# A macaron block on one core: the longest attention row turned by 32x32 squares and DMA instead of on TensorE

## The reference, cut to what matters

```python
x = x + 0.5 * ffn(layernorm(x))
x = x + attn(layernorm(x))
x = x + 0.5 * ffn(layernorm(x))

def attn(h):                       # h: 8 x 512 x 512
    q = h @ w_q.T                  # 16 heads of 32
    k, v = split(h @ w_kv.T)       # one key and one value head of 32 for all
    q, k = rotate(q / sqrt(32)), rotate(k / sqrt(32))
    p = softmax(where(causal, -inf, q @ k.T))
    return (p @ v) @ w_proj.T + b_proj
```

## Time and profile before

| what | value |
|---|---|
| median of three runs | 2725.27 us |
| profiled execution, time | 2725.83 us |
| profiled execution, span | 2724.0 us |
| granted TensorE clock, mean | 0.999 |
| TensorE busy | 2686.4 us, 99% |
| VectorE busy | 1877.6 us, 69% |
| ScalarE busy | 1117.9 us, 41% |
| GpSimd busy | 305.9 us, 11% |
| attention, first to last step | 1089.8 to 1660.0 us |

### The profile page before, as it was taken

The page is one execution under the profiler, slowest core; times in us unless marked ns, Lnnn a source line. Parts: engine busy times, 40 slices in busy tenths (PEclk is TensorE's granted clock), DMA queues, the critical chain, the costliest instruction groups (busy, mean ns, idle before and its releaser), DMA issues.

```text
span 2724.0 us, 41269 instructions
## 1 busy us (share of the span) xinstructions
PE 2686.4 (99%) x15328; PEld 2170.4 (80%) x15328; DVE 1877.6 (69%) x3538; ACT 1117.9 (41%) x2376; POOL 305.9 (11%) x318
## 2 busy tenths in 40 slices
PE   8999999999999999999999999999999999999999
PEld 6888888888888887677777767888888888888887
DVE  6667766766686667777777775667766776677655
ACT  4333333333333333877777774333333333333332
POOL 0000000000000004544444420000000000000000
PEclk9999999999999999999999999999999999999999
DMA  4211411331132111000000012212321242123100
GB/s 141 88 49 56 162 47 46 95 123 47 46 124 93 47 46 59 20 17 27 30 32 29 29 56 86 81 50 78 112 78 58 70 135 82 46 60 126 47 16 31
DMA packets 96747, 181.63 MB, mean 67 GB/s; under 512 B 7744, under 2 KB 32576, under 8 KB 96320
## 3 DMA queue, kind: packets, MB, share of 16 engines
q1 hardware_dynamic: 96576, 179.34, 19.6%
HBM read 141.56 MB, written 37.75 MB: 66 GB/s over the span
## 4 chain that ended last, share of the span: by engine, by line
PE 94%; DVE 4%; ACT 1%; POOL 1%; issue 1%; DMA 0%; SPq 0%; DVEq 0%; ACTq 0%; POOLq 0%
PE bank L457 50%; PE bank L478 25%; PE bank L1199 5%; PE bank L1167 3%; PE bank L1190 3%; PE bank L1214 3%; PE bank L1227 3%; DVE probs L1449 1%; PE bank L1142 1%; PE bank L1175 1%; PE bank L335 1%; POOL xnt_l L1072 0%; DVE pt L1455 0%; PE bank L494 0%; DVE att L1468 0%
## 5 line engine op out<-in xcount | busy, mean ns | idle before, releaser
L457 PE MATMUL bank<-xnt_h,wgu_h 128*128 128x512 f32 x2048 | 799.0, 390 | 4.4 <-ACT sg L575 2.8
L457 PE MATMUL bank<-xnt_h,wgu_l 128*128 128x512 f32 x2048 | 797.6, 389 | 1.0 <-issue 1.0
L457 PE MATMUL bank<-xnt_l,wgu_h 128*128 128x512 f32 x2048 | 797.7, 390 | 0.0
L650 DVE TENSOR_TENSOR h<-bank,sg 128x512 f32<-128x512 f32 x256 | 176.7, 690 | 544.1 <-PE bank L457 530.4
L457 PEld LDWEIGHTS bank<-xnt_h,wgu_h 128*128 128x128 f32 x2048 | 385.0, 188 | 87.3 <-ACT sg L575 3.7
L457 PEld LDWEIGHTS bank<-xnt_h,wgu_l 128*128 128x128 f32 x2048 | 385.0, 188 | 80.1
L457 PEld LDWEIGHTS bank<-xnt_l,wgu_h 128*128 128x128 f32 x2048 | 385.1, 188 | 79.6
L579 ACT ACTIVATE mag<-h 128x512 f32<-128x512 f32 x256 | 162.0, 633 | 674.5 <-DVE h L650 674.5
L478 PE MATMUL bank<-wd_h,hs_h 128*128 128x512 f32 x1008 | 392.2, 389 | 0.0
L478 PE MATMUL bank<-wd_h,hs_l 128*128 128x512 f32 x1008 | 392.1, 389 | 0.0
L478 PE MATMUL bank<-wd_l,hs_h 128*128 128x512 f32 x1008 | 392.1, 389 | 0.0
(11 more groups left out here) (137 smaller groups left out, 3196.5 us busy)
## 6 DMA issues: line engine op xcount, KB each, us to landing
raw_gu<-in_w_gu SPq DMA_DIRECT2D x128, 512.0 KB, 4.9
raw_d<-in_w_d SPq DMA_DIRECT2D x128, 256.0 KB, 2.6
x_mid<-x_sb SPq DMA_DIRECT2D x64, 256.0 KB, 2.1
x_squares<-xs SPq DMA_DIRECT2D x48, 256.0 KB, 3.9
xs<-x_squares SPq DMA_DIRECT2D x12, 1024.0 KB, 5.6
x_sb<-x_mid SPq DMA_DIRECT2D x10, 1024.0 KB, 5.5
x_sb<-in_x SPq DMA_DIRECT2D x32, 256.0 KB, 4.2
out<-x_sb SPq DMA_DIRECT2D x32, 256.0 KB, 2.1
```

What stands on the lines that cost most here:

```text
L457: last = pe.matmul(ps, w[:, r, kind, k], xs[:, b, k], start=(i == 0), stop=(i == 3 * KD - 1))
L650: v.tensor_tensor(h[:, r], bank[UP + r % 2][:, :], sg[:, r % 2], ALU.mult).then_inc(h_done, 1)
```

## The change

Row 3, the longest, becomes the first of each group (`ORDER` is 3, 0, 1, 2, and the unit of row 3 is at steps 0, 4, 8 and 12). Its blocks are no longer turned on TensorE and copied. VectorE writes its masked scores to `probs3` in pieces of 32 columns, turns the 32x32 squares of two heads at a time in place (`turn_squares`), and the tile goes to DRAM (`squares`) in four transfers of 256 KB and comes back in one of 1 MB as `pt3`. Two of the four are issued by SyncE and two by ScalarE. ScalarE waits for both turns and, from the second group on, for the previous read back before it issues. SyncE issues the read after all four have landed and after the previous group's weighing.

The other three rows get a buffer each. VectorE does all four masks first in a step, and copies one block a group instead of four; ScalarE copies five instead of six. TensorE weighs once a group, in the step of the next long row. Some projections, statistics and the turn of the keys stand in other steps. GpSimd splits x tiles earlier in a step. SyncE's stores and loads of x are woven between the groups. In the second phase `inside` is called after the first gate and after the first up bank, with the last weighing at the first and the last output projections at the second.

```diff
+    squares = nc.dram_tensor("squares", [S // 32, 32, TT, HG * 32], F32, kind="Internal").ap()
...
-    pt = place("pt", [P, 2 * TT, HG, P], F32)
+    pt = place("pt", [P, 6, HG, P], F32)
+    probs1 = place("probs1", [P, HG, 2 * P], F32)
...
-    probs = place("probs", [P, 3, HG, S], F32)
+    probs3 = place("probs3", [P, S // 32, HG, 32], F32)
+    pt3 = place("pt3", [P, TT, TT, HG, 32], F32)
+    probs2 = place("probs2", [P, HG, 3 * P], F32)
+    probs0 = place("probs0", [P, HG, P], F32)
...
-                            if inside and r == kind == 0:
+                            if inside and r == 0:
...
-            ORDER = (0, 1, 2, 3)
-            PLACES = ((7,), (5, 6), (0, 1, 2), (3, 4, 5, 6))
-            ON_VECTOR = ((), (1,), (1,), (1, 3))
-            TURN_X, TURN_KV, TURN_K = {11: 0, 12: 1, 13: 2, 14: 3}, 1, 4
+            ORDER = (3, 0, 1, 2)
+            LONG = 3
+            PLACES = ((0,), (1, 2), (3, 4, 5))
+            ON_VECTOR = ((), (), (1,))
+            probs_of = (probs0, probs1, probs2)
+            TURN_X, TURN_KV, KEYS, TURN_K = {11: 0, 12: 1, 13: 2, 14: 3}, 1, 8, 10
...
-            FIRST_PROJECT = {0: ("kv", 0), 1: ("q", 0), 5: ("q", 1), 9: ("q", 2), 10: ("q", 3)}
-            LAST_PROJECT = {2: ("out", 0), 5: ("out", 1), 9: ("out", 2), 13: ("out", 3)}
-            STATS = {3: 0, 5: 1, 7: 2, 8: 3}
+            FIRST_PROJECT = {0: ("kv", 0), 2: ("q", 0), 5: ("q", 1), 6: ("q", 2), 10: ("q", 3)}
+            LAST_PROJECT = {2: ("out", 0), 6: ("out", 1), 10: ("out", 2), 14: ("out", 3)}
+            STATS = {3: 0, 4: 1, 5: 2, 7: 3}
...
+            def store_squares(engine, a):
+                engine.dma_start(squares[:, :, a].rearrange("c i x -> i c x"),
+                                 probs3[a * 32:(a + 1) * 32, :, :, :].rearrange("p c s n -> p c (s n)")).then_inc(squares_stored, 16)
...
+                def turn_long(G):
+
+                    if G > 0:
+                        sp.wait_ge(pt3_loaded, G * 16)
+                    sp.wait_ge(squared, (G + 1) * 2)
+                    for a in range(TT // 2):
+                        store_squares(sp, a)
+                    sp.wait_ge(squares_stored, (G + 1) * TT * 16)
+                    if G > 0:
+                        sp.wait_ge(pv_done, G)
+                    sp.dma_start(pt3[:, :, :, :, :].rearrange("p j a s n -> p j (a s n)"),
+                                 squares.rearrange("(j q) i a x -> (q i) j (a x)", q=TT)).then_inc(pt3_loaded, 16)
...
+                for B in range(BATCHES):
+                    for hg in range(NHG):
+                        turn_long(B * NHG + hg)
...
+                    if B > 0:
+                        store(B - 1)
+                    if 0 < B < BATCHES - 1:
+                        sp.wait_ge(ax_stored, B * TT * 16)
+                        load(B + SLOTS - 1)
...
+                    pe.wait_ge(pt3_loaded, (G + 1) * 16)
+                    for i in ORDER:
+                        if i == ORDER[1]:
+                            pe.wait_ge(pt_scalar, blocks_before(K, by_scalar))
+                            pe.wait_ge(pt_vector, blocks_before(K, by_vector))
+                        for j in range(i + 1):
+                            for s in range(HG):
+                                turned = pt3[:, j, :, s, :] if i == LONG else pt[:, PLACES[i][j], s]
...
-                    if k % 2 == 0 and K > 0:
-                        weigh(K - 2)
-                        weigh(K - 1)
+                    if k % TT == 0 and K > 0:
+                        weigh(K // TT - 1)
                     if K + AHEAD < ALL:
                         scores(K + AHEAD)
...
+                    if k % TT == 0:
+                        if K > 0:
+                            a.wait_ge(pt3_loaded, K // TT * 16)
+                        a.wait_ge(squared, (K // TT + 1) * 2)
+                        for quarter in range(TT // 2, TT):
+                            store_squares(a, quarter)
                     if k % TT == 0 and K > 0:
                         drain_sums(K // TT - 1)
                     exps(K + 1, 2)
-                    copy_turned(K, 0)
+                    if 0 in mine:
+                        copy_turned(K, 0)
                     exps(K + 1, 3)
+                    if 1 in mine:
+                        copy_turned(K, 1)
...
+                def turn_squares(K, pair):
+
+                    if K >= ALL:
+                        return
+                    v.wait_ge(exp_done, K * HG + 2 * pair + 2)
+                    pieces = probs3[:, :, 2 * pair:2 * pair + 2, :].rearrange("p c s n -> p c (s n)")
+                    v.transpose(pieces, pieces).then_inc(squared, 1)
...
-                    mask_scores(K + AHEAD - 1, (0, 1))
-                    if 1 in ON_VECTOR[i]:
+                    mine = () if i == LONG else ON_VECTOR[i]
+                    mask_scores(K + AHEAD - 1, range(HG))
+                    if k % TT == TT - 1:
+                        turn_squares(K + 1, 0)
+                    if 1 in mine:
                         copy_turned(K, 1)
-                    mask_scores(K + AHEAD - 1, (2, 3))
-                    if nxt < BATCHES and k == TURN_KV + 1:
+                    if k % TT == TT - 1:
+                        turn_squares(K + 1, 1)
+                    if nxt < BATCHES and k == KEYS:
                         keys(nxt)
```

More of the change, by code:

```diff
@@ L75, in macaron_kernel @@
     rstd = place("rstd", [P, NB, TT], F32)
-    nmax = place("nmax", [P, 3, TT], F32)
+    nmax = place("nmax", [P, TT, TT], F32)
     sums = place("sums", [P, 2, HG, TT], F32)
@@ L926, in att_of, with blocks_of, row_of_head, in_pieces @@
                 return (xnt_h[:, 1], xnt_l[:, 1]) if B % 2 == 1 else (att2_h[:, :, :], att2_l[:, :, :])
-            def heads_of(ap):
-                return ap.rearrange("p (h d) -> p h d", d=HD)
+            def blocks_of(i):
+                return 0 if i == LONG else i + 1
+            def row_of_head(K, s):
+                i = row_of(K)
+                return probs3[:, :, s, :] if i == LONG else probs_of[i][:, s, :]
+            def in_pieces(ap):
+                return ap.rearrange("p (c n) -> p c n", n=32)
             def blocks_before(K, of):
-                one = [sum(1 for j in range(i + 1) if of(i, j)) for i in ORDER]
+                one = [sum(1 for j in range(blocks_of(i)) if of(i, j)) for i in ORDER]
                 return K // TT * sum(one) + sum(one[:K % TT])
@@ L967, in attention_phase @@
                 nxt = B + 1
-                next_turn("p", K, 0)
-                if row_of(K) >= 1:
-                    next_turn("p", K, 1)
+                for j in range(min(blocks_of(row_of(K)), 2)):
+                    next_turn("p", K, j)
                 if k in project_in(B):
@@ L973, in attention_phase @@
                     next_turn(*(("out", B - 1, t) if what == "out" else ("kv", nxt) if what == "kv" else ("q", nxt, t)))
-                for j in range(2, row_of(K) + 1):
+                for j in range(2, blocks_of(row_of(K))):
                     next_turn("p", K, j)
@@ L1010, in sync @@
                 yield
+                def turn_long(G):
[9 more added lines that the diff above has]
+                                 squares.rearrange("(j q) i a x -> (q i) j (a x)", q=TT)).then_inc(pt3_loaded, 16)
                 load(2)
                 load(3)
[L1013 to L1021, removed]
-                store(BATCHES - 2)
+                for B in range(BATCHES):
+                    for hg in range(NHG):
+                        turn_long(B * NHG + hg)
+                        if B == BATCHES - 1 and hg == 0:
+                            sp.wait_ge(q_finished, BATCHES * NHG)
+                            load_raw(0)
+                            sp.wait_ge(k_step, BATCHES * KSTEP)
+                            sp.wait_ge(x_biased, BATCHES * TT)
+                            load_raw(1)
+                    if B > 0:
[3 more added lines that the diff above has]
+                        load(B + SLOTS - 1)
                 sp.wait_ge(proj_done, (BATCHES - 1) * TT)
@@ L1078, in step @@
                         part_output(K // TT - 1)
+                    if nxt + 1 <= BATCHES and k - 1 in TURN_X:
+                        part_x(nxt + 1, TURN_X[k - 1])
                     if k % TT == 2:
@@ L1244, in step @@
                     B, k = divmod(K, UNITS)
-                    i, nxt = row_of(K), B + 1
-                    turn_probs(K, 0)
-                    if i >= 1:
-                        turn_probs(K, 1)
+                    blocks, nxt = blocks_of(row_of(K)), B + 1
+                    for j in range(min(blocks, 2)):
+                        turn_probs(K, j)
                     project(B, k)
-                    for j in range(2, i + 1):
+                    for j in range(2, blocks):
                         turn_probs(K, j)
@@ L1326, in exps @@
                     G, i = K // TT, row_of(K)
-                    row = probs[:, K % 3, s, 0:width(i)]
```

(5 more changed lines are left out.)

50 lines of the change are left out of this document (26 added, 24 removed).

## The result

The changed kernel takes 2710.53 us (median of five runs, 2707.34 to 2716.26), the kernel before 2725.27: a ratio of 0.9949 [0.9934, 0.9963], 14.7 us less. Forecast were 35 us less. The profiled execution is the slowest of the five, 2716.26 us with a span of 2714.5; 9.5 us less than the span before.

The account below looks back on a forecast made before the run. TensorE was taken as the bound: from the profiled 2725.8 us, 69.0 go on TensorE and 33.6 of waits for VectorE come, giving 2690.4, or 2690 for the runs. The forecast case's range was 2675 to 2708, the whole range 2655 to 2735.

Parts of the forecast that it names:

- The bound: Whole kernel: TensorE is 94% of the chain that ended last; time is won only where it works or waits less.
- What goes: Attention, TensorE: the long row's transposes, 63.0 us in 32 groups, and step 15's bank wait, 6.0; together 69.0 us less.
- What comes on VectorE: Attention: turns and masks on VectorE make TensorE wait 4.2 us a batch, 33.6 in all; ends 0 and 64.
- the walk: Steps 5 to 8 of a batch, timed by engine: TensorE waits 1.9 us for masks before the 384-column scores.
- ScalarE (a small part): Two store issues per group on ScalarE, between 0.86 and 2.83 us, taken as 1.4: hidden from TensorE.
- Rival B: ScalarE held 2.83 us by its issues instead of 1.4; three groups a batch lose 1.2, 29 us, 2719; chance 0.17.
- The round trip: Squares to DRAM and back: 7.4 us to the read's issue, 5.6 to landing, 13.0; hidden, slack 1.5 or more.
- Rival D: Squares come back late and the weighing waits, for instance 2 us a group, 64 us: about 2754; chance 0.07.
- A: TensorE gets no new wait because VectorE hides everything: 2656 to 2665 us; chance 0.15.
- C: Granted clock falls in TensorE's new waits in three groups of every batch; chance 0.14.

## Why the prediction was partly right

- **The bound (right for six batches of eight).** "TensorE is 94% of the chain", so "time is won only where TensorE works less or waits less". True in the inner batches and the seventh: 73.8 to 70.1 and 69.15, where the forecast was 69.4. Averaged over the kernel it hid that the first batch had 5 us without TensorE, and the last 4.2 (61.17 - 56.98). The row was on the table, and I gave it no term.
- **What goes (the step that failed).** 32 x 1.97 + 7 x 0.86 = 69.0 was taken off the kernel's time one for one, in all eight batches. The kernel with small turns, where the other side of the sum is nearly gone (an eighth of the turns and ScalarE's issues remain), shows 47. An inner batch gave 7.5 of 8.6 and the last 8.1, 1.7 of it weighing that only moved out; the first gave nothing, with either table (66.75 and 65.6 us, before 65.7), and that is the largest piece of the 22 missing. The 7 x 0.86 did go from step 15, but a wait of the same size came in step 11 (6.6 us in seven places), where the turns delay the copy of a bank.
- **What comes on VectorE (right in sum, by luck in part).** "That is 4.2 a batch, 8 x 4.2 = 33.6 us", and the turns cost 32.5. In an inner batch the walk held in its main lines: 3.8 us, of it twice 1.32 where it said 1.9, and 0.86 and 0.36 before x tiles where it said 0.4. But it leant on its last sentence there, "After that TensorE has a step with a projection, and VectorE catches up". In the outer batches that isn't so: of the 16 steps, five and four hold a projection. The new tables leave steps 1, 9 and 13 of the first batch without one, and steps 1, 5, 9 and 13 of the last. There the turns cost 5.4 and 11.9 in the profiled execution; with the old tables 3.2 and 2.4.
- **Both together.** Each batch was to give 4.4 us. In the profiled execution 26 us of the forecast are missing (20 by the medians): 19 in the first and last batch, which took 5.9 with the seventh (200.3 to 206.2) where the three were to give 13.2; 4 in the five inner ones; 3 outside.
- **The tables and the ends (missed).** I named the moved projections but gave them no term. They cost 13.7 us in the kernel before, and 5.4 in the change. The last weighing moved in the lists and the long row put first were costed at nothing too; run-up and end are 1.1 and 1.0 us longer.
- **ScalarE (a small part).** 1.4 us an issue pair was taken; it is 0.9 in most groups and about 2 in the others, and in the group shown the exponentials are 1.09 late, as priced at 1.2 for 2.83, and TensorE's longest wait for one is 1.8. Rival B's mechanism is real for 4 us of the kernel, its price of 29 is not.
- **The round trip (right).** From the first store to the read back's issue 5.6 in the median where 7.4 was taken (10.1 at worst), landing 5.5 for 5.6, no wait of a weighing. Rival D is out for the change. With one queue and the later turn it came up once, and its kin, masks waiting for stores, in 26 places.
- **Rivals A and C.** A is out by the waits. C stood for a granted clock that falls in TensorE's new waits in three groups of every batch; its chance of 0.14 and the range's end at 2735 come from that, and no run shows it. In the inner batches the clock was 1.00 with the waits of 1.32 us; it fell in the outer ones (0.88 and 0.87), and giving it back was worth 2 us.
- **The statement of what would show it** (an inner batch of 69 to 70, TensorE busy under 96% of it, waits after nmax before the 384-column scores, 768 transposes) came out: 70.1 us, 325.66 / 350.67 = 93%, 1.32 us, and 768 in the trace. None of these looked at an outer batch.

Open: what bounds the first batch near 65.6 us, which it keeps even with small turns and old tables (VectorE's maxima are what TensorE waits for most there, 7.1 us, but no run takes them away); and why the issues of stores are held in some groups and not in others.

## What to carry to other kernels

Divide a stage before spreading a term over it: with small turns the saving on the busiest engine came to 7.5 of 8.6 us in an inner batch, where it had 1.3 us of idle time, and to nothing in the first, where it had 5. Work moved to a second engine costs by where the next result for the first one stands in its order, so try it behind that result (5.7 us here, with two queues), and place the covering work (here projections) ahead of it (5.4 us). Don't issue transfers from an engine on which others wait, if one with nothing to do has time for them (4.2 us).

## What the runs showed of the hardware that was not expected

- Two issues of 256 KB stores took 0.91 us on ScalarE's queue in most groups, and 1.3 to 2.4 in nine of 32, in seven of them at the same moment as SyncE's (2.42 and 2.43 us in one). The groups differ from run to run. The changed kernel's times spread over 8.9 us, other kernels' with two queues over 2.5 to 8.8 and with one queue over 1.3 to 4.7; that the holds make the spread is not shown.
- Twelve of sixteen transposes taken out of a stretch of 1.97 us left 1.66, with waits of 0.46 and 0.33 for banks that were still being copied out.
- Filling matmuls raised the granted clock from 0.88 to 0.96 in the first batch, and the kernel's time fell by 2 us of 2710, within its scatter.
- After a wait of 1.95 us the 80 weighing matmuls took 4.03 us instead of 2.39, at a granted clock of 0.57.
